# 16-head attention of four sequences: two blocks of two sequences, against one pipeline in slots with two-part stacks

## The reference, cut to what matters

```python
x = x + attn_a(_layernorm(x), w_qkv, b_qkv, w_proj, b_proj)   # 16 heads of 8 features
x = x + ffn(_layernorm(x), ...)      # two layers: windowed attention and gated MLP
x = x + attn_b(_layernorm(x), ...)   # linear attention
x = x + ffn(_layernorm(x), ...)

def attn_a(x, w_qkv, b_qkv, w_proj, b_proj):
    qkv = (x @ w_qkv + b_qkv).reshape(b, n, 3, 16, 8).transpose(2, 0, 3, 1, 4)
    q, k, v = qkv
    attn = softmax(einsum('bhnd,bhmd->bhnm', q, k) * 8 ** -0.5)
    out = einsum('bhnm,bhmd->bhnd', attn, v).transpose(0, 2, 1, 3).reshape(b, n, 128)
    return out @ w_proj + b_proj
```

## Time and profile before

| | us |
|---|---|
| median of three runs (1187.47 to 1193.08) | 1191.71 |
| the profiled execution | 1192.93 |
| its span, first to last instruction | 1191.1 |
| PE busy | 1000.9 (84%) |
| DVE busy | 827.9 (70%) |
| ACT busy | 718.4 (60%) |
| POOL busy | 391.0 (33%) |
| mean granted clock of TensorE | 0.925 of full speed |

### The profile page before, as it was taken

How to read it: one execution, slowest core, us unless ns; L and a number is a source line. 1 busy time by engine, 2 the same in 40 slices (tenths; PEclk the granted TensorE clock), 3 DMA queues, 4 the chain that set the end, 5 groups by cost and what they waited for, 6 DMA issues and landing times.

```text
span 1191.1 us, 22117 instructions
## 1 busy us (share of the span) xinstructions
PE 1000.9 (84%) x8272; PEld 595.0 (50%) x8272; DVE 827.9 (70%) x1381; ACT 718.4 (60%) x1500; POOL 391.0 (33%) x251
## 2 busy tenths in 40 slices
PE   5079997248997589999999889888889999999996
PEld 3023324112323466666766556656566667667662
DVE  4078824347863687988988767767777898888861
ACT  3027773106784477687777656656574876777762
POOL 5000006000000755544554424243334455455420
...
DMA packets 38268, 36.01 MB, mean 30 GB/s; under 512 B 11478, under 2 KB 30224, under 8 KB 38160
## 3 DMA queue, kind: packets, MB, share of 16 engines
...
## 4 chain that ended last, share of the span: by engine, by line
PE 48%; DVE 11%; issue 3%; ACT 3%; POOL 2%; DVEq 0%; POOLq 0%
PE psum L1162 7%; PE psum L1094 5%; PE psum L1134 5%; PE psum L1037 4%; PE psum L1073 4%; PE psum L1170 3%; PE psum L1047 3%; PE psum L1039 3%; PE psum L1038 3%; PE psum L1083 3%; DVE f_NM L1424 2%; DVE f_A L1392 2%; PE psum L1106 2%; DVE f_BS L1396 2%; DVE f_SS L1403 2%
## 5 line engine op out<-in xcount | busy, mean ns | idle before, releaser
L966 POOL TENSOR_TENSOR f_A<-f_A,f_BS 128x1024 f32<-128x1024 f32 x64 | 151.0, 2359 | 219.5 <-DVE f_BS L1396 219.2
L500 DVE TENSOR_REDUCE a_M<-psum 128x1 f32<-128x512 f32 x256 | 159.9, 683 | 63.1 <-PE psum L430 62.9
L430 PE MATMUL psum<-a_KS,a_QS 128*128 128x512 bf16 x256 | 104.9, 419 | 76.1 <-DMA a_KS<-minus_ones 73.8
L547 ACT ACTIVATE a_PT<-psum 128x1024 f32<-128x1024 f32 x128 | 126.4, 1018 | 52.5 <-PE psum L452 52.0
L971 POOL TENSOR_TENSOR f_A<-f_A,f_RN 128x1024 f32<-128x1024 f32 x64 | 121.9, 1904 | 107.7 <-ACT f_RN L1282 107.0
L1271 ACT ACTIVATE f_PW<-psum,f_NM 128x128 f32<-128x128 f32 x512 | 138.9, 382 | 14.0 <-DVE f_NM L1424 10.9
L1237 ACT ACTIVATE f_SQ<-psum 128x512 f32<-128x512 f32 x128 | 75.9, 609 | 84.2 <-PE psum L1039 79.6
L1392 DVE TENSOR_TENSOR f_A<-psum,cos 128x512 f32<-128x512 f32 x128 | 87.8, 686 | 48.0 <-ACT f_SQ L1237 47.9
L1424 DVE TENSOR_REDUCE f_NM<-psum 128x4 f32<-128x512 f32 x128 | 81.9, 680 | 55.1 <-PE psum L1073 55.1
L430 PEld LDWEIGHTS psum<-a_KS,a_QS 128*128 128x128 bf16 x256 | 25.4, 100 | 157.5 <-DMA a_KS<-minus_ones 74.2
L452 PE MATMUL psum<-a_QS,a_KS 128*128 128x512 bf16 x256 | 94.9, 389 | 8.2 <-DMA a_QS<-a_MROW 7.2
...
## 6 DMA issues: line engine op xcount, KB each, us to landing
...
```

What stands on the lines that cost most here:

```text
L430: nc.tensor.matmul(psum[:, take("tile", 8 * unit + k), :], QS[:, n, h + k // 4, P * qt:P * qt + P], KS[:, n, h + k // 4, :], start=True, s ...
L500: nc.vector.tensor_reduce(M[:, u % 4, k // 4, k % 4:k % 4 + 1], psum[:, bank("tile", i), :], AX_X, ALU.max)\
L547: nc.scalar.activation(PT[:, head % 8, 2 * (half % 2):2 * (half % 2) + 2, :], psum[:, SLOT[i % 2][0]:SLOT[i % 2][1] + 1, :], ACT.Exp, scal ...
L966: nc.gpsimd.tensor_tensor(A[:, k % 2, :, :], A[:, k % 2, :, :], BS[:, k % 2, :, :], ALU.add)\
```

## The change

`attention_a` is one block for all four sequences. Its work is cut into slots: a slot holds the score product of two heads for 128 queries ("scores", S) and, 14 slots later (`E_LAG`), the product by key of two heads for 128 keys ("by_key", B). A sequence has 32 slots, a quad of heads 8. All other pieces of work are hung on slots by the table `AROUND` (offset from the sequence's first slot, name, quad), and `slots_a` writes out one plan that every engine walks through in the same order.

- Stacks: queries and keys are split into two parts, high and low, in fp32r by GpSimd (L397, L399), and products with 0/1 matrices (`SELECT`) place them in 24 rows a head, four heads in the four row groups of 32. ScalarE copies the query stack (L595), VectorE the key stack while it adds the guard row's -1 (L641). Nothing goes through memory but the rows of maxima (L358).
- Maxima: one reduction over two banks (L648) instead of two over one.
- Banks: six banks are three pairs that S and B take in turn (`take_pair`), so that a product waits for the reader of the third product before it; the last two banks serve all single pieces in turn.
- Denominators: a product with a 0/1 matrix spreads each over its head's rows (L532), then comes a reciprocal of 128x512 on VectorE (L654) and a product on GpSimd (L405). The projection is four products with zero-padded weights (L539); the value bias goes into the output bias.
- Norms: variance by a product with ones, then Ln and Exp on ScalarE; no other activation table is loaded.

```diff
-NB = 2
-RUNS = [(0, 2), (0, 1), (0, 0), (1, 2), (2, 2)]
-LAG = 3
...
-            for pair in range(SEQS // NB):
-                attention_a(nc, g, pair)
+            attention_a(nc, a, g)
...
-def attention_a(nc, g, pair):
...
-        QS = sb("QS", [P, NB, HA, T], BF16)
-        KS = sb("KS", [P, NB, HA, T], BF16)
...
+E_LAG = 14
...
+AROUND = sorted([(-32, "turn_x", 0), (-29, "center_x", 0), (-27, "var_x", 0), (-21, "queries_keys", 0),
+                 (-3, "values", 0), (-16, "stack", 0), (-13, "stack", 1), (-11, "stack", 2), (-5, "stack", 3),
+                 *((8 * quad + 9, "maxima", quad) for quad in range(QUADS)),
+                 *((8 * quad + 22, "sums", quad) for quad in range(QUADS)),
+                 *((8 * quad + 23, "sums_2", quad) for quad in range(QUADS)),
+                 *((8 * quad + 26, "spread", quad) for quad in range(QUADS)),
+                 (52, "project", 0), (56, "center_y", 0), (60, "var_y", 0)])
...
+def slots_a():
+    plan = []
+    for slot in range(AROUND[0][0], SEQS * SLOTS + AROUND[-1][0] + 1):
+        if 0 <= slot < SEQS * SLOTS:
+            plan.append(("scores", slot))
+        if 0 <= slot - E_LAG < SEQS * SLOTS:
+            plan.append(("by_key", slot - E_LAG))
+        for n in range(SEQS):
+            for at, work, quad in AROUND:
+                if SLOTS * n + at == slot:
+                    plan.append((work, QUADS * n + quad if work in PER_QUAD else n))
+    return plan
...
+    def pair(work, i):
+        return slice(2 * (pair_at[work, i] % 3), 2 * (pair_at[work, i] % 3) + 2)
+    def bank(work, i):
+        return 6 + at[work, i] % 2
...
+    FREED = {"scores": (("maxed", lambda i: i + 1),), "by_key": (("exped", lambda i: i + 1),),
+             "bias": (("bias_made", lambda i: 1),), "turn_x": (("x_copied", lambda i: i + 1),),
...
+             "maxima": (("row_made", lambda i: i + 1),), "sums": (("o_copied", lambda i: i + 1),),
+             "spread": (("den_recip", lambda i: i + 1),), "project": (("x_added", lambda i: i + 1),)}
...
+        QH = sb("QH", [P, 2, T], F32R)
+        QL = sb("QL", [P, 2, T], F32R)
...
+        QS = sb("QS", [P, 2, QUADS, T], F32R)
+        KS = sb("KS", [P, 2, QUADS, T], F32R)
...
+        PT = sb("PT", [P, 8, 4, T])
+        OC = sb("OC", [P, 2, T])
+        RD = sb("RD", [P, T])
+        ON = sb("ON", [P, QUADS, T])
...
+                    elif work == "maxima":
+                        n, quad = i // QUADS, i % QUADS
+                        sp.wait_ge(s("row_made"), i + 1)
+                        for j in range(4):
+                            sp.dma_start(QS[32 * j + ROWS_T:32 * j + ROWS_E, n % 2, quad, :].bitcast(F32),
+                                         MROW[j:j + 1, i % 2, :].bitcast(F32))\
+                              .then_inc(s(f"row_in{i % 2}"), 16)
+                        for dst, src in todo[:8]:
+                            load(dst, src, "weights")
+                        todo = todo[8:]
...
+                        for w in range(2):
+                            pool.wait_ge(s("biased"), 2 * n + w + 1)
+                            nc.gpsimd.tensor_copy(QH[:, w, :], QF[:, w, :]).then_inc(s("high"), 1)
+                            pool.wait_ge(s("high"), 2 * n + w + 1)
+                            nc.gpsimd.tensor_tensor(QL[:, w, :], QF[:, w, :], QH[:, w, :].bitcast(F32), ALU.subtract)\
+                                .then_inc(s("low"), 1)
+                    elif work == "spread":
+                        pool.wait_ge(s("den_recip"), n + 1)
+                        if n >= QUADS:
+                            pool.wait_ge(s("project"), n // QUADS)
+                        nc.gpsimd.tensor_tensor(ON[:, n % QUADS, :], OC[:, n % 2, :], RD[:, :], ALU.mult)\
+                            .then_inc(s("divided"), 1)
...
+                def take_pair(work, i):
+                    x = pair_at[work, i]
+                    if x >= 3:
+                        freed(*pairs[x - 3])
+                    return psum[:, pair(work, i), :]
+                def take(work, i):
+                    x = at[work, i]
+                    if x >= 2:
+                        freed(*singles[x - 2])
+                    return psum[:, bank(work, i), :]
...
+                def weighted_sums(i, tiles):
+                    n, quad = i // QUADS, i % QUADS
+                    dst = psum[:, bank("sums", i), :]
+                    for kt in tiles:
+                        pe.wait_ge(s("exped"), 8 * i + 4 + kt + 1)
+                        for j in range(4):
+                            last = nc.tensor.matmul(dst[32 * j:32 * j + 32, :], VA[:, n % 2, kt, 4 * quad + j, :],
+                                                    PT[:, (4 * i + j) % 8, kt, :], start=(kt == 0), stop=(kt == 3))
+                    return last
...
+                    elif work == "stack":
...
+                        for w, kind in enumerate(("q_stack", "k_stack")):
+                            pe.wait_ge(s("low"), 2 * n + w + 1)
+                            dst = take(kind, i)
+                            nc.tensor.matmul(dst, SELECT[rows, 2 * w, :], QH[rows, w, :], start=True, stop=False)
+                            last = nc.tensor.matmul(dst, SELECT[rows, 2 * w + 1, :], QL[rows, w, :], start=False,
+                                                    stop=True)
+                            last.then_inc(s(kind), 1)
...
+                        dst = take_pair("scores", i)
+                        for h in range(2):
+                            rows = slice(32 * (2 * j + h), 32 * (2 * j + h) + ROWS_T)
+                            last = nc.tensor.matmul(dst[:, h, :], QS[rows, n % 2, quads % QUADS, P * t:P * t + P],
+                                                    KS[rows, n % 2, quads % QUADS, :], start=True, stop=True)
+                        last.then_inc(s("scored"), 1)
...
+                        if j == 0 and t == 0:
+                            pe.wait_ge(s(f"row_in{quads % 2}"), 64 * (quads // 2 + 1))
+                        dst = take_pair("by_key", i)
+                        for h in range(2):
+                            rows = slice(32 * (2 * j + h), 32 * (2 * j + h) + ROWS_E)
+                            last = nc.tensor.matmul(dst[:, h, :], KS[rows, n % 2, quads % QUADS, P * t:P * t + P],
+                                                    QS[rows, n % 2, quads % QUADS, :], start=True, stop=True)
+                        last.then_inc(s("scored_by_key"), 1)
...
+                    elif work == "sums":
+                        if i % QUADS == 0:
+                            pe.wait_ge(s("v_copied"), i // QUADS + 1)
+                        take("sums", i)
+                        weighted_sums(i, (0, 1))
+                    elif work == "sums_2":
+                        weighted_sums(i, (2, 3)).then_inc(s("summed"), 1)
+                    elif work == "spread":
+                        pe.wait_ge(s("o_copied"), i + 1)
+                        nc.tensor.matmul(take("spread", i), cst("spread"), OC[:, i % 2, :], start=True, stop=True)\
+                          .then_inc(s("spread"), 1)
...
+                        pe.wait_ge(s("divided"), QUADS * (i + 1))
+                        dst = take("project", i)
+                        for quad in range(QUADS):
+                            last = nc.tensor.matmul(dst, WP[:, quad, :], ON[:, quad, :], start=(quad == 0),
+                                                    stop=(quad == QUADS - 1))
+                        last.then_inc(s("project"), 1)
...
+                    elif work == "by_key":
+                        n, quads, j, t = heads(i)
+                        if j == 0 and t == 0 and quads >= 2:
+                            act.wait_ge(s("summed"), quads - 1)
+                        act.wait_ge(s("scored_by_key"), i + 1)
+                        h = (4 * quads + 2 * j) % 8
+                        nc.scalar.activation(PT[:, h:h + 2, t, :], psum[:, pair("by_key", i), :], ACT.Exp,
+                                             scale=float(DA) ** -0.5).then_inc(s("exped"), 1)
+                    elif work == "sums_2":
+                        act.wait_ge(s("summed"), i + 1)
+                        if i >= 2:
+                            act.wait_ge(s("divided"), i - 1)
+                        nc.scalar.activation(OC[:, i % 2, :], psum[:, bank("sums", i), :], ACT.Copy)\
...
+                        n, quads, j, t = heads(i)
+                        if j == 0 and t == 0 and quads >= 2:
+                            dve.wait_ge(s("maxima"), quads - 1)
+                        dve.wait_ge(s("scored"), i + 1)
+                        nc.vector.tensor_reduce(M[:, quads % 2, t, 2 * j:2 * j + 2], psum[:, pair("scores", i), :],
+                                                AX_X, ALU.max).then_inc(s("maxed"), 1)
+                    elif work == "spread":
+                        dve.wait_ge(s("spread"), i + 1)
+                        if i:
```

(3 more changed lines are left out.)

680 lines of the change are left out of this document (270 added, 410 removed).

## The result

| | before | after |
|---|---|---|
| median of 5 runs, us | 1191.46 (1187.47 to 1193.08) | 1197.95 (1197.52 to 1200.4) |
| ratio to before | | 1.0062, 95% interval 1.0035 to 1.0090 |
| span of the profiled execution, us | 1191.1 | 1195.5 |
| mean granted clock | 0.925 | 0.895 |

A forecast was written before the change was run, and what follows sets the result against it. TensorE bounds the head loops now, transfers the two holes. Attention takes 29 + 18 + 261 + 16 + 23 = 347 us instead of 385.3, 38 less: 1192.9 - 38 = 1155 us; range 1118 to 1200.

The forecast's parts named there:

- the term for TensorE's clock: Slots 14 to 127: half speed behind reciprocal holes costs 0 to 1.1 us a quad, more at projections; 13 us taken.
- rival 3: Middle slots: 6 us or more at half speed behind each hole slows both sums halves; 46 us, 1201 us; chance 0.17.
- 3.4 us a hole: Middle slots: after a gap of 3.32 us TensorE runs at 1.2 GHz for some 3.4 us.
- VectorE's waits in front of the maxima: Slots 14 to 127: two slots with half the sums each leave VectorE idle, together 3.0 us a quad.
- Rival 2: Score products: pairs run one behind the other, and tile-shape visits cost 0.4 us, not 0.2; 1172 us; chance 0.15.
- Rival 1: Middle slots: VectorE's work sets the pace, ring free; 189 us instead of 261, 1083 us, half gain 1119; chance 0.12.
- The estimate of 4.4 us: Reciprocal of 128x512 on VectorE: 8.3 ns a column by the skill, about 1168 us; the forecast used 3.4 us.
- Rival 4: Transfers of rows of maxima behind weights in SP's queue hold B: some 6 us, 1161; within the forecast's 0.56.
- The beginning: Loads, dependent preparation chain and first stacks up to the first maximum: 29 us, against 61.9 now.
- The last exponentials: Slots 128 to 141, exponentials only: 14 us and 2 for a late row of maxima, 16 us.
- The end: Chain from last sums to norm: 18.2 us, and 5 for the clock, 23 us.
- 2.29 us a slot: Cost of a slot in the new kernel, paid where 1.78 us are needed now.

The follow-up runs named there:

- e16: Repetition of e10, all 128 rows in the real pairs against after, attention's result left out: 1190.85 us, 1.0012.
- the twins: Kernel pairs differing in six added products, 24 or 128 rows: on after 1210.53 (e9) and 1183.25 us; on e2 1196.27 and 1170.33 us.
- e1: After, with twelve added 24-row score products in each of slots 3 and 4 of every eight: 1211.46 us, 1.0195.
- e9: After, with six added 24-row products, all in one row tile, in each of the slots of e1: 1210.53 us, 1.016.
- e12: After, with a product of 128 rows and 64 columns between the two pairs of every slot from 3 on: 1255.55 us, 1.0535.
- e2: After, with the reciprocal moved from VectorE to ScalarE as Ln and Exp: 1161.08 us, 0.977.
- e10: After, with all 128 rows in the real pairs instead of row tiles, attention's result left out: 1191.17 us, 0.9987.
- e11: e2 with all 128 rows in the real pairs instead of row tiles, attention's result left out: 1141.14 us, 0.9571.

## Why the prediction was wrong

**The step that failed** is the term for TensorE's clock, "I take 13 us in all". It rested on two readings: that the clock falls only behind the hole of each reciprocal, for some 3.4 us, and (against rival 3) that TensorE, 60 to 70% busy outside the holes, would hold it. In the run the middle was at half speed for about half of its time with TensorE busy 243 of 295 us. The clock fell and stayed low while TensorE worked on row-tiled pairs of 24 and 25 rows, sometimes before the hole, and it rose with added products of 128 rows that did nothing but run. The reading of 3.4 us a hole came from the stream of the kernel before, where the products behind those holes have 128 rows (701.68 to 706 us, shows the first); e16, with 128 rows in the pairs, keeps it, 4.4 us a fall, and after, with row tiles, takes 10.0. 3.4 us in each of 14 quads are some 48 us at half speed; the run had about 150. The price was right, 13 us for 48 being 0.27 against the twins' 0.26 to 0.32; the amount was not. The 100 us more are 26 to 32 us at that price, and 34 were missing in the middle. That is an estimate: no run had row tiles and a full clock, and within after the quads with more half speed are not clearly the longer ones, since their pieces differ.

**Rival 3** was the nearest: 1201 us, slower, by the clock, with both halves of the sums at half speed. Its number was right within 3 us and its sign as well; its chance, 0.17, was too small. Its mechanism was half right. The clock did it, but not by the holes: e1 and e9 filled them and gained nothing. So it is in part luck that its number fits: the clock's share is some 26 to 32 us of the 44, not all of them. The range, 1118 to 1200, held the time.

**VectorE's waits in front of the maxima** were given 3.0 us a quad for the two halves of the sums; in the quad shown they are 3.68 and 1.13, and all waits for score products come to 81.6 us. The maxima themselves were forecast right: one lasts 1213 ns, and where nothing holds them they start 1.13 us apart (three in 3.47 us at 52.54). Only a maximum that follows a wait has no neighbour to overlap with. The additions behind the three projections waited 14.4 us, 4.8 each where 2.9 had been taken.

**Rival 2** was half right too. The pairs run side by side, so its first half fell. Its second, 0.4 instead of 0.2 us a visit, is what the trace and e12 (0.38 to 0.46) show. The 86 visits could thus be up to 17 us of the loss; how many lie beside VectorE's work isn't settled.

**Rival 1** fell in its strong form: the middle was nowhere near 189 us. Yet VectorE's reciprocal was worth 37 of its 54 us (after to e2) or 50 (e10 to e11), with some 7 to 9 us of clock in each: the one large piece that the forecast had right, nothing hid it. The estimate of 4.4 us, which the prediction worked out from the repeat count of 8 in the Trainium skill (VectorE: DVE Perf Modes, the 8-slice walkthrough), did not come: it took 3357 ns, 6.4 ns a column more behind the 558 of 64 columns, as the rows of before had it.

**Rival 4** did not come: TensorE's waits for rows of maxima come to 2.5 us between 54 and 360 us of after (the weight loads of L513).

**The beginning and the end.** First maximum at 33.8 us instead of 29. The stacks of the first sequence go through two single banks and take 2.1 us a quad, not 0.9, since each waits for the copy of the one before:

```profile
25.64 0.89 PE L491 MATMUL psum<-a_QH,a_SELECT 32*128 32x512 f32 x2 [0.80 <-DVE a_KS L641]
...
27.77 0.89 PE L491 MATMUL psum<-a_QH,a_SELECT 32*128 32x512 f32 x2 [0.81 <-DVE a_KS L641]
```

The last exponentials took 21.3 us instead of 16, because the two halves of one quad's sums still stand between them, the first at half speed:

```profile
356.72 3.64 PE L443 MATMUL psum<-a_PT,a_VA 128*32 128x512 f32 x16
360.29 0.79 PE L513 MATMUL psum<-a_QS,a_KS 25*128 25x512 f32 x2
361.01 2.33 PE L443 MATMUL psum<-a_PT,a_VA 128*32 128x512 f32 x16
```

The forecast had left them out of that stage. The end was right, 21.8 for 23, and so was what goes: both holes and the serial ends. (The 2.29 us a slot in the prediction's sum hold for slots 14 to 127; over all 128 it comes to 2.18, and that is what balances its 38 us.)
